# A two-layer cross-attention kernel: context and bias columns loaded in transposed layout, first splits spread over three engines, new order of loads and first products

## The reference

```python
def _cross_attention(q_in, kv_in, wq, bq, wk, bk, wv, bv, wo, bo, bias_k, bias_v):
    qh = (q_in @ wq + bq).reshape(b, q_len, H, K)        # H = 16 heads, K = 128
    kh = (kv_in @ wk + bk).reshape(b, t, H, K)
    vh = (kv_in @ wv + bv).reshape(b, t, H, K)
    kh, vh = kh with one more token bias_k, vh with one more token bias_v
    weights = jax.nn.softmax(einsum('bqhk,bthk->bhqt', qh, kh) / sqrt(K))
    return einsum('bhqt,bthk->bqhk', weights, vh).reshape(b, q_len, H * K) @ wo + bo

x = x + _cross_attention(layer_norm(x), ctx, ...layer 1...)
x = x + _cross_attention(layer_norm(x), ctx, ...layer 2...)
out = x + gelu(layer_norm(x) @ w_fc1 + b_fc1) @ w_fc2 + b_fc2
```

## Time and profile before

| | us |
|---|---|
| median of 3 runs (lowest to highest) | 497.98 (497.58 to 499.17) |
| the profiled execution, its own time | 496.78 |
| its span, first to last instruction | 495.0 |

### The profile page before, as it was taken

The page is one execution under the profiler, slowest core; times in us unless marked ns, Lnnn a source line. Parts: engine busy times, 40 slices in busy tenths (PEclk is TensorE's granted clock), DMA queues, the critical chain, the costliest instruction groups (busy, mean ns, idle before and its releaser), DMA issues.

```text
span 495.0 us, 11021 instructions
## 1 busy us (share of the span) xinstructions
PE 489.1 (99%) x3228; PEld 444.5 (90%) x3228; DVE 391.2 (79%) x911; ACT 331.0 (67%) x727; POOL 413.7 (84%) x387
## 2 busy tenths in 40 slices
PE   8999999999999999999999999999999999999997
PEld 6888998998998998999988989999989989999997
DVE  4889877888878878866789888788788888766896
ACT  3777767667775866666486877758666677768441
POOL 4877989989898998997597999989989898999542
PEclk9999999999999999999999999999999999999999
DMA  7435886756667676612115786676767566650001
GB/s 272 149 104 170 265 249 197 208 187 195 187 195 209 192 229 190 181 58 66 42 44 164 267 236 184 203 199 202 222 189 209 181 195 179 206 156 1 23 23 42
DMA packets 52901, 82.56 MB, mean 167 GB/s; under 512 B 5882, under 2 KB 33934, under 8 KB 52878
## 3 DMA queue, kind: packets, MB, share of 16 engines
q1 hardware_dynamic: 52878, 82.28, 54.5%
HBM read 53.42 MB, written 28.84 MB: 166 GB/s over the span
## 4 chain that ended last, share of the span: by engine, by line
PE 91%; DVE 6%; DMA 1%; POOL 1%; ACT 1%; issue 0%; DVEq 0%; POOLq 0%
PE ring L1190 68%; PE ps_ctx L1190 11%; PE acc L1190 9%; PE ring L1236 1%; DVE v_lo L1174 1%; DVE k_hi L1172 1%; DVE k_lo L1174 1%; DMA probs<-ctx_in 1%; DVE v_hi L1172 1%; DVE h_lo L971 0%; DVE pT_lo L890 0%; PE ring L1545 0%; DVE z_sb L951 0%; PE ring L1273 0%; DVE k_lo L825 0%
## 5 line engine op out<-in xcount | busy, mean ns | idle before, releaser
L905 DVE TENSOR_REDUCE row_max<-ring 128x1 f32<-128x512 f32 x112 | 76.1, 688 | 27.8 <-PE ring L1190 27.7
L634 ACT ACTIVATE probs<-ring,shift 128x512 f32<-128x512 f32 x112 | 76.4, 682 | 18.9 <-DVE shift L910 18.8
L415 POOL TENSOR_TENSOR v_lo<-v_sum,v_hi 128x512 fp32r<-128x512 f32 x64 | 82.9, 1297 | 2.7 <-ACT v_hi L584 2.7
L868 DVE STREAM_TRANSPOSE blocks<-probs 128x512 f32<-128x512 f32 x108 | 70.1, 687 | 4.9 <-POOL probs L422 4.6
L422 POOL TENSOR_SCALAR probs<-probs,inv 128x512 f32<-128x512 f32 x80 | 55.2, 696 | 20.3 <-DVE inv L918 20.2
L427 POOL TENSOR_TENSOR pT_lo<-wf_lo,pT_hi 128x1024 fp32r<-128x1024 f32 x28 | 67.0, 2412 | 0.0
L1190 PE MATMUL ring<-pT_lo,v_hi 128*128 128x256 f32 x208 | 58.4, 281 | 0.2 <-DVE pT_lo L890 0.2
L566 ACT ACTIVATE k_hi<-ring,cols 128x512 fp32r<-128x512 f32 x57 | 37.8, 688 | 31.0 <-PE ring L1190 30.8
L1190 PE MATMUL ring<-pT_hi,v_lo 128*128 128x256 f32 x208 | 58.1, 279 | 0.0
L1190 PE MATMUL ring<-pT_hi,v_hi 128*128 128x256 f32 x208 | 58.0, 279 | 0.0
L1190 PE MATMUL ring<-wv_lo,cT_hi 128*128 128x256 f32 x196 | 54.8, 279 | 0.0
(11 more groups left out here) (208 smaller groups left out, 1631.8 us busy)
## 6 DMA issues: line engine op xcount, KB each, us to landing
spill<-blocks SPq DMA_DIRECT2D x54, 512.0 KB, 2.9
wf_lo<-spill SPq DMA_DIRECT2D x112, 128.0 KB, 3.2
wf_hi<-spill SPq DMA_DIRECT2D x104, 128.0 KB, 3.2
wk_raw<-wk_in SPq DMA_DIRECT2D x17, 256.0 KB, 2.8
wq_raw<-wq_in SPq DMA_DIRECT2D x17, 256.0 KB, 3.4
wv_raw<-wv_in SPq DMA_DIRECT2D x16, 256.0 KB, 3.7
vrows<-vrows_in SPq DMA_DIRECT2D x16, 256.0 KB, 4.0
wo_raw<-wo_in SPq DMA_DIRECT2D x16, 256.0 KB, 2.7
```

Source lines behind the costliest of these rows:

```text
L415: pool.tensor_tensor(v_lo[:, 2 * m:2 * m + 2, :], v_sum[:, m % 2, :].rearrange("p (t c) -> p t c", c=PW), v_hi[:, 2 * m:2 * m + 2, :].bitc ...
L634: act.activation(probs[:, u, q, :], ring[S_BANKS[where][QTB * u + q]][:], ACT.Exp, bias=shift[:, u, q:q + 1], scale=SCALE, accum_out=row_s ...
L868: last = dve.transpose(blocks[:, u % 2, :, :, q, :].rearrange("p g c b -> p c g b"), probs[:, u, q, :].rearrange("p (c g b) -> p c g b", g ...
L905: dve.reduce_max(row_max[:, u, q:q + 1], ring[S_BANKS[where][QTB * u + q]][:], AX_X).then_inc(max_done, 1)
```

## The change

The host now hands over the context transposed (dimension on the partitions, token along the row), so that it lands as TensorE needs it, in four loads of one (batch, half of the dimensions) each, and all constants' columns in one load `all_cols`. The transposes, the copies of columns, and their semaphores go. WARM_UP is 8 instead of 5.

The loads come in this order: wk, context (0,0), context (0,1), wv, x of batch 0, columns, wq, vrows, context (1,0), context (1,1), x of batch 1; then the second wk behind `wk_split`, the second wv with vrows behind `wv_split` and the new `vbias_ready`, the second wq behind `wq_split`, then wo and out_rows, then the two parts of the MLP.

The high parts of wk and wq are made by POOL, that of wv by ACT; the low parts of all three by VectorE. The low part of batch 1's context is made by POOL (`late_c`), and so is z of batch 1 (`late_z`). TensorE makes both key tiles of batch 0 together, then both value tiles, then z's transposes, then both key tiles of batch 1 and the queries; the tile banks of the second value tile and of the fourth key tile differ from before. Batch 1's key tiles reuse the bank of the first, hence the wait for `k_split` 1.

```diff
-V_BANKS = {... "prologue": [3, 5], ...}
-K_BANKS = {... "prologue": [5, 4, 0, 1]}
+V_BANKS = {... "prologue": [3, 1], ...}
+K_BANKS = {... "prologue": [5, 4, 0, 5]}
-WARM_UP, KEEP_WARM = 5, 2
+WARM_UP, KEEP_WARM = 8, 2
@@ block.sync
-            for b in range(BATCH):
-                sp.dma_start(c_raw[:, CTB * b:CTB * (b + 1), :], ctx_in[b].rearrange("(p t) d -> p t d", t=CTB)).then_inc(c_loaded[b], LOAD)
-                if b == 0:
-                    load_wk(0)
-                    sp.dma_start(head_rows[:], head_rows_in).then_inc(rows_loaded, LOAD)
-                    sp.dma_start(dim_rows[:], dim_rows_in).then_inc(rows_loaded, LOAD)
...
+            def load_c(b, c):
+                j = DC * b + c
+                sp.dma_start(c_raw[:, b, c, :], ctx_in[:, CLEN * j:CLEN * (j + 1)]).then_inc(c_loaded[j], LOAD)
...
+            load_wk(0)
+            load_c(0, 0)
+            load_c(0, 1)
+            load_value_weight(0)
+            load_x(0)
+            sp.dma_start(all_cols[:], cols_in).then_inc(cols_loaded, LOAD)
             load_wq(0)
-            load_wo(0)
-            sp.dma_start(out_rows[:], ...)
+            load_vrows(0)
+            load_c(1, 0)
+            load_c(1, 1)
+            load_x(1)
             sp.wait_ge(wk_split, 1)
             load_wk(1)
             sp.wait_ge(wv_split, 1)
+            sp.wait_ge(vbias_ready, 1)
             load_wv(1)
             sp.wait_ge(wq_split, 1)
             load_wq(1)
+            load_wo(0)
+            sp.dma_start(out_rows[:], ...)
@@ block.gpsimd
-            split_wk(0)
-            pool.wait_ge(cols_copied, 2)
+            pool.wait_ge(wk_loaded, LOAD)
+            pool.tensor_scalar(wk_hi[:], wk_raw[:], 1.0, 0.0, ALU.mult, ALU.add).then_inc(wk_rounded, 1)
+            pool.wait_ge(cols_loaded, LOAD)
...
+            def late_c(c):
+                pool.wait_ge(cT_rounded, DC + c + 1)
+                pool.tensor_tensor(cT_lo[:, c, CLEN:], c_raw[:, 1, c, :], cT_hi[:, c, CLEN:].bitcast(F32), ALU.subtract).then_inc(cT_split_late, 1)
...
                 if layer == 0:
+                    pool.wait_ge(wq_loaded, LOAD)
+                    pool.tensor_scalar(wq_hi[:], wq_raw[:], 1.0, 0.0, ALU.mult, ALU.add).then_inc(wq_rounded, 1)
                     inverse_deviation(0, 0)
                     value_bias(0)
-                    split_wv(0)
-                    split_wq(0)
+                    late_c(0)
+                    late_c(1)
                     inverse_deviation(0, 1)
-                    pool.wait_ge(z_ready, QT)
+                    pool.wait_ge(z_ready, QTB)
+                    late_z()
@@ block.scalar
+            round_c(0, 0)
+            round_c(0, 1)
+            act.wait_ge(wv_loaded, LOAD)
+            act.activation(wv_hi[:], wv_raw[:], ACT.Copy).then_inc(wv_rounded, 1)
             act.wait_ge(cols_ready, 1)
             round_k(0, 0, "prologue")
+            round_k(0, 1, "prologue")
...
-                    round_k(0, 1, "prologue")
-                    round_k(0, 2, "prologue")
+                    round_c(1, 0)
+                    round_c(1, 1)
                     drain_h(0, 0)
                     round_h(0, 0)
+                    round_v(0, 0)
+                    round_k(0, 2, "prologue")
                     round_k(0, 3, "prologue")
-                    round_v(0, 0)
@@ block.vector
+            first_rest(wk_raw, wk_hi, wk_lo, wk_rounded, wk_split)
             split_c(0)
             split_c(1)
...
+            first_rest(wv_raw, wv_hi, wv_lo, wv_rounded, wv_split)
             stats(0, 0)
-            split_c(2)
-            split_c(3)
+            first_rest(wq_raw, wq_hi, wq_lo, wq_rounded, wq_split)
...
                     standardise(0, 0)
+                    dve.wait_ge(vbias_ready, 1)
+                    sum_v(0, 0, where)
+                    split_k(0, 0, where)
                     stats(0, 1)
-                    split_k(0, 0, where)
+                    split_h(0, 0)
+                    sum_v(0, 1, where)
                     split_k(0, 1, where)
                     split_k(0, 2, where)
-                    split_h(0, 0)
-                    dve.wait_ge(wv_split, 1)
-                    sum_v(0, 0, where)
-                    standardise(0, 1)
-                    split_k(0, 3, where)
                     split_first_q(0, 0, 0, layer)
                     split_first_q(0, 1, 0, layer)
-                    sum_v(0, 1, where)
+                    split_k(0, 3, where)
@@ block.tensor
+            def first_keys(b):
+                part = slice(b * CLEN, (b + 1) * CLEN)
+                tiles = [(ring[K_BANKS["prologue"][2 * b + h]][:], slice(h * HD, (h + 1) * HD)) for h in range(2)]
+                def rest(c):
+                    for out, heads in tiles:
+                        last = pe.matmul(out, wk_hi[:, c, heads], cT_lo[:, c, part], start=False, stop=c == DC - 1)
...
                 for c in range(DC):
+                    if b == 0 and c == 0:
+                        pe.wait_ge(wk_rounded, 1)
                     pe.wait_ge(cT_rounded, DC * b + c + 1)
+                    for out, heads in tiles:
+                        pe.matmul(out, wk_hi[:, c, heads], cT_hi[:, c, part], start=c == 0, stop=False)
+                    if b == 0 and c == 0:
+                        pe.wait_ge(wk_split, 1)
+                    for out, heads in tiles:
+                        pe.matmul(out, wk_lo[:, c, heads], cT_hi[:, c, part], start=False, stop=False)
+                    if b == 0:
+                        pe.wait_ge(cT_split, c + 1)
+                        rest(c)
+                if b == 1:
+                    for c in range(DC):
+                        pe.wait_ge(cT_split_late, c + 1)
+                        rest(c)
...
                 if layer == 0:
-                    transpose_z(0, 0, where)
-                    project_k(3, where)
+                    first_keys(0)
                     pe.wait_ge(wv_split, 1)
                     project_v(0, where)
+                    project_v(1, where)
+                    pe.wait_ge(ident_ready, 2)
+                    transpose_z(0, 0, where)
+                    pe.wait_ge(k_split, 1)
+                    first_keys(1)
...
                     pe.wait_ge(k_split, 2)
                     transpose_z(0, 1, where)
-                project_v(1, where)
-                if layer > 0:
+                else:
+                    project_v(1, where)
                     transpose_z(layer, 1, where)
...
                 scores(0, 0, "first")
+                if layer == 0:
+                    pe.wait_ge(v_summed, NV * pair + 2)
                 scores(0, 1, "first")
                 pe.wait_ge(q_split, NQ * (pair + layer + 1))
                 pe.wait_ge(v_summed, NV * pair + 2)
+                pe.wait_ge(k_split, NK * pair + 3)
                 scores(1, 0, "first")
...
-            pe.wait_ge(ident_ready, 2)
-            transpose_c(0)
-            pe.wait_ge(rows_loaded, 2 * LOAD)
-            pe.transpose(ring[4][:, 0:P], head_rows[:], ident[:])
-            pe.transpose(ring[4][:, P:P + 20], dim_rows[:], ident[0:20, 0:20]).then_inc(cols_filled, 1)
-            first_keys()
-            transpose_c(1)
-            pe.wait_ge(cols_copied, 2)
-            project_k(1, "prologue")
-            late_keys(2)
```

More of the change, by code:

```diff
@@ L50 @@
 C_BANKS = {"step": [2, 0, 2, 5], "last": [2, 1, 0, 2], "own": [4, 1, 3, 4]}
-V_BANKS = {"first": [None, None, 3, 0], "step": [5, 4, 0, 1], "last": [5, 0, 1, 3], "prologue": [3, 5], "between": [3, 0]}
-K_BANKS = {"first": [4, 1, 5, 3], "step": [1, 3, 2, 3], "last": [2, 2, 1, 5], "prologue": [5, 4, 0, 1]}
+V_BANKS = {"first": [None, None, 3, 0], "step": [5, 4, 0, 1], "last": [5, 0, 1, 3], "prologue": [3, 1], "between": [3, 0]}
+K_BANKS = {"first": [4, 1, 5, 3], "step": [1, 3, 2, 3], "last": [2, 2, 1, 5], "prologue": [5, 4, 0, 5]}
 FIRST_Q_BANKS = [2, 4]
@@ L174, in build_program @@
         ident_ready, zeros_ready = sem("ident_ready"), sem("zeros_ready")
[L175 to L176 removed]
+        cT_rounded, cT_split, cT_split_late = sem("cT_rounded"), sem("cT_split"), sem("cT_split_late")
+        cols_ready, cols_moved = sem("cols_ready"), sem("cols_moved")
         x_ready, bn_done, stats_ready = sem("x_ready"), sem("bn_done"), sem("stats_ready")
@@ L364, in value_bias @@
             def value_bias(n):
-                pool.wait_ge(wv_loaded, (2 * n + 2) * LOAD)
-                pool.tensor_tensor(vbias[:], vrows[:, 0, :], vrows[:, 1, :], ALU.subtract)
+                pool.wait_ge(vrows_loaded, (n + 1) * LOAD)
+                pool.tensor_tensor(vbias[:], vrows[:, 0, :], vrows[:, 1, :], ALU.subtract).then_inc(vbias_ready, 1)
             def split_wv(n):
+                hold(wv_loaded, (n + 1) * LOAD)
                 split_tile(wv_raw[:], wv_hi[:], wv_lo[:], wv_rounded, n + 1, wv_split)
@@ L1275, in transpose_z @@
                 last.then_inc(h_filled, 1)
-            def first_keys():
```

(34 more changed lines are left out.)

77 lines of the change are left out of this document (36 added, 41 removed).

## The result

The changed kernel takes **500.5 us** (median of 12 runs, 499.02 to 502.16) against 498.08 for the kernel before (12 runs, 496.76 to 499.75): a ratio of 1.005, with a 95% interval of 1.0036 to 1.0064. It is slower; 495.9 was forecast, 497.9 was the top of the range. The profiled execution took 501.95 us with a span of 500.1, against 496.78 and 495.0.

What follows compares the result with a forecast made beforehand. TensorE, nearly gapless, was taken as the bound, so only time before the first score product counted: 19.70 to 17.6, 2.1 us less, making 494.7 profiled and, 1.2 above, a 495.9 us median. Range 494.2 to 497.9.

Steps and rivals of the forecast that it cites:

- part 2: Prologue start: warm-up ends at 5.1 us; at lags of 0.5 to 0.8 the context lands at 4.0 and 4.8.
- Part 5: POOL and VectorE chain before second keys: k_lo done at 11.8 us, TensorE waiting 0 to 0.5 us.
- rival B: Before the deviation, POOL waits for wq, delaying z, second keys and scores; 1.6 us lost, 497.5 us, chance 0.15.
- Rival C: Late x of batch 1 holds VectorE and h_lo before the queries; landing at 17 gives 500.3 us, chance 0.1.
- part 3: First splits on three engines: VectorE's low parts are not late for TensorE; contention beside POOL charged at nothing.
- Late z on POOL: Batch 1's standardisation before the queries: two tiles at 0.37 to 0.70 us each, 15.7 at worst, covered.
- Part 4: First keys, values and z on TensorE: keys end at 8.5 us, values at 11.3, z transposes at 11.7.
- the waits that I placed at 11.7: TensorE before its second keys: waiting for k_lo, 0 to 0.5 us, in place of the h_lo wait.
- The new wait for q_lo: TensorE in front of the scores: a wait of 1.1 us made by the reordering.
- Queries to scores: From the start of the queries at 14.55 us to the first score product: 3.05 us.
- What lies behind the first score product: Rest of the kernel: shifted earlier by the same 2.1 us, within 0.3.
- The list of signs: Proof against: scores after 18.6, POOL standing for wq beyond 8.5, x1 read after 13, TensorE idle over 1 us in 19 to 41.

Runs made afterwards that it cites:

- E1: Changed kernel with each of the four context loads stored as one contiguous block; 498.79 us, ratio 1.0027 to the kernel before.
- E6: E1 with the load of the columns moved from sixth to second place; 498.9 us, ratio 1.0008 to the kernel before.
- e10: e7 with the context strided as in the changed kernel, so the order edit alone; 498.33 us, ratio 1.0009 to the kernel before.
- e2: Changed kernel with SP waiting for the second context load before issuing wq, vrows and the rest; 498.86 us, ratio 1.002 to the kernel before.
- e7: E1 with x0 loaded before wv, deviation first on POOL, statistics and z earlier on VectorE, k_lo before v_sum; 496.85 us, ratio 0.9967.
- e9: E1 with columns third, x0 before wv, deviation before wq_hi on POOL, VectorE making k_lo before z and both late z; 496.48 us, ratio 0.9974.
- e4: Changed kernel with ten warm-up products instead of eight; 499.58 us, ratio 1.0034 to the kernel before.
- e3: Changed kernel with seven products of zeros on TensorE, four before z's transposes and three behind; 499.84 us, ratio 1.0041 to the kernel before.
- e8: e7 with wq, wk and wv also stored so that each load is one block; 496.96 us, ratio 0.9977 to the kernel before.
- e5: Changed kernel with the edits of E1 and e3 together; 497.93 us, ratio 0.9986 to the kernel before.

## Why the prediction was wrong

**The step that failed is the landing times of part 2.** I took lags from 0.5 to 0.8 us on the rate of before, 324 to 335 GB/s, and gave that rate to context loads that in the new layout take 2 KB out of each 8 KB row. The first half of the context moved at 176 to 205; all behind it (wv, x0, columns, wq) came 2.6 to 3 us late. E1 gives 1.35 of the lost microseconds back.

**Part 5 was the right list of links and the wrong bound.** I saw that deviation and z stand behind the columns and wq on POOL, and priced that as rival B, "each us by which wq lands after 7.7 moves z, v_sum, k_lo, second keys and scores by one". So it went, but with the columns in wq's place: they are late by 2.75, wq lands at 10.3 and finds POOL still busy with them, and the second keys (16.24) are late by 4.4. B had 0.15, and a size of 1.6 us from one lag; the sign turns from a landing 2.1 late, which I did not say. Nor did part 5 say that the statistics of x, behind wv_lo on VectorE, are as late as POOL (11.17 beside 11.23). E6 shows that the columns' load alone is not it, e10 that the order of the chain is worth 1.25 us; how much of that is POOL's list and how much VectorE's stays open. Rival C, x1, did not decide: it landed at 13.0, and its statistics began at 16.11, behind k_lo.

**Shared interfaces, charged at nothing in part 3, cost.** The nearest rows said little and pointed to 0.70 for z; seen are var_eps 0.19 to 0.70 beside wq_lo, z 1.98 for two tiles, wq_lo 1.22 and 1.77 beside POOL. z follows what POOL does beside it: 1.98 with vbias and the late context rests, 1.02 in e2, where it has only vbias beside it, 0.74 in e7, beside the small column operations. The rule that I set against the change (the Trainium skill, GPSIMD Engine Reference, Specifications: contention between VectorE and GpSimd for the shared SBUF interfaces, where a VectorE instruction has two SBUF inputs) is borne out for wq_lo, which has two: 0.69 in after, 1.22 in e7, 1.77 in e9. Late z on POOL took 1.22 a tile where 0.37 to 0.70 was estimated; that looks like the price of the operation there and not of the neighbour, for it is 2.43 or 2.44 for two in every profile that shows both. It stayed "covered" all the same: in e7 PE waits 0.71 for it, but inside the time in which it would have waited for q_lo.

**Part 4, the middle of two pitches.** I took 8.5 for the end of the keys between 7.9 and 9.2. The fast pitch began at 10.15, 2.4 us later than the 7.7 I had assumed. Whether the pause of 0.65 us in front of the keys did it stays open. Without a pause it begins at 5.7 to 7.3 (five profiles); with eight warm-up products and a pause of 0.6 us or more at 9.3 to 10.4 in four, but in e6 and e10, with pauses of 1.02 and 1.19, the keys are fast from the first. In any case keys ending early only wait for z and k_lo (e4).

**A loss of the granted clock was in no case of mine.** It costs 1.7 us in 7 of 12 executions. I had the two levels in view at the start and did not ask what the waits that I placed at 11.7 would do to the level behind them. The trace shows 1.03 us of work in 2.80 us and then 0.50 for 3.0 us; filled with seven products of zeros (e3) the fall is gone in 8 of 9.

**What held.** The transposes are gone. The new wait for q_lo was put at 1.1 us and measured 1.06. Queries to scores took 3.08 for 3.05. What lies behind the first score product follows within the scatter, 475.3 to 476.7 us in 14 profiles, though in the two first ones it differs by 1.04 where I had allowed 0.3. The list of signs worked too: scores after 18.6 and PE idle for over 1 us in 19 to 41 were named as proof against it; POOL stood until 9.7 as well, but for the columns and not for wq, and x1 was read at 16.11, though it had landed at 13.0.

**What stays open.** By the profiles e7, e8 and e9 reach the first score product only 0.35 to 0.65 us before the first profile of before (1.0 at most before its second), but their medians are 1.2 to 1.7 us lower; single profiles cannot settle more. Why 2 KB rows at 8 KB apart are slow and ones at 34.8 KB are not was not tried. Nor was e9 with the columns behind the whole context, or without the wait for q_lo, which now stands in front of the scores in every version.

## What to carry to other kernels

Time taken off the bound engine counts only if its next inputs arrive as much earlier: before crediting it, write down for each in-order engine which load stands in front of the chain that the bound engine will wait for, and put the chain first (1.25 us here). Price a load by its own layout, not by the rate of its neighbours (1.35 us here), and a task moved to VectorE or POOL by its duration on that engine and beside the other. Before you take a listed wait for a cost, look at what the same instruction needs besides: the 0.71 us for late z in e7 lie inside the wait for q_lo. A wait placed on TensorE can cost a second time, by the lower clock of what follows.

## What the runs showed of the hardware

- 128 rows of 2 KB, 8 KB apart: 176 and 205 GB/s; in one contiguous block: 352 and 340, same queue and time (3 to 5 us: 135 to 206 in six profiles, 255 to 346 in four). 34.8 KB apart: at most 0.4 us later than in a block.
- In the changed kernel wv, x0, the columns, wq and vrows were seen 6.6 to 7.0 us after their issue, the 74 KB of columns as late (6.65) as the 262 KB loads around them. With the context in blocks (e1) wv, x0, columns and wq took 4.7 to 5.1.
- VectorE and POOL beside each other: POOL's 128x2 operation 0.19 to 0.70, its 128x32 one 0.25 to 0.55; VectorE's 128x512 difference of two SBUF operands 0.69 to 1.22 and 1.77; its standardisation of 256 columns 0.37 to 0.99 (mean of two; the longest single one 1.35). Standardisation on POOL, 1.22 us a tile wherever it is made there, against 0.62 for its rounding of 512 columns.
- The granted clock fell to 0.50 behind a stretch where PE worked 1.03 of 2.80 us and no single wait was longer than 0.82. The mean is 0.997 in 12 of 20 executions of the changed kernel, with seven products of zeros in that stretch in 1 of 9, and in none of 55 of e5 and e7 to e10 (three of those list 0.999).
- The time at which matmuls of 512 columns go from 0.43 to 0.23 us apart at the start varied from 5.7 (e9) to 10.4 us (e3) between profiles with the same eight warm-up products; the column of the clock shows 1.00 through the slow ones too.
